# One Softplus activation for the step size of a selective scan, and more outer products on GpSimd

## What is computed

```python
x_dbl = einsum('bsd,ed->bse', u, x_proj_w)           # u: 1024 channels after convolution and silu
dt_r, B, C = split(x_dbl, [64, 80], axis=-1)
dt = softplus(einsum('bsr,dr->bsd', dt_r, dt_proj_w) + dt_proj_b)
A = -exp(A_log)                                       # 1024 x 16
def step(h, inp):                                     # over the tokens
    dt_t, B_t, C_t, u_t = inp
    h = h * exp(dt_t[:, :, None] * A) + (dt_t * u_t)[:, :, None] * B_t[:, None, :]
    y = einsum('bdn,bn->bd', h, C_t)
    return h, y
y = (ys + u * D_param) * silu(z)
x = x + gate * einsum('bse,de->bsd', y, out_proj_w)
```

## Time and profile before

| | |
|---|---|
| median of 3 runs | 2315.27 us |
| lowest and highest run | 2314.59 and 2320.24 us |
| profiled execution: span from first to last instruction | 2313.7 us |
| first layer's units | about 69 to 1815 us of the span |
| TensorE, VectorE, ScalarE, GpSimd busy | 93%, 89%, 69%, 77% |
| granted TensorE clock, mean | 0.96 |

### The profile page before, as it was taken

How to read it: one execution, slowest core, us unless ns; L and a number is a source line. 1 busy time by engine, 2 the same in 40 slices (tenths; PEclk the granted TensorE clock), 3 DMA queues, 4 the chain that set the end, 5 groups by cost and what they waited for, 6 DMA issues and landing times. The chain is left out here.

```text
span 2313.7 us, 30061 instructions
## 1 busy us (share of the span) xinstructions
PE 2147.8 (93%) x9984; PEld 1411.3 (61%) x9984; DVE 2049.7 (89%) x2258; ACT 1607.2 (69%) x3119; POOL 1775.3 (77%) x1048
## 2 busy tenths in 40 slices
PE   9889989988998899899989988998868899999999
PEld 3345555555555555555555555555545599988888
DVE  4899999999999999999999999999999666666666
ACT  3677787887787778777877887787666355566655
POOL 0587899999999999999999999999999422132225
PEclk9889999999999999899999999999978899999999
DMA  6611231151124111421321141114101210112113
GB/s 223 252 39 51 95 134 42 55 175 50 46 52 169 51 55 42 178 91 51 124 99 48 55 178 38 46 54 167 38 22 58 89 35 26 38 57 60 40 55 128
DMA packets 86137, 191.17 MB, mean 83 GB/s; under 512 B 8350, under 2 KB 11678, under 8 KB 85983
## 3 DMA queue, kind: packets, MB, share of 16 engines
q1 hardware_dynamic: 85982, 189.25, 24.7%
HBM read 171.91 MB, written 17.30 MB: 82 GB/s over the span
## 5 line engine op out<-in xcount | busy, mean ns | idle before, releaser
L1460 POOL TENSOR_TENSOR arena<-arena 128x1024 f32<-128x1024 f32 x512 | 1199.9, 2362 | 116.8 <-ACT arena L622 114.7
L1057 DVE TENSOR_TENSOR_SCAN arena<-ps,arena 128x512 f32<-128x512 f32 x1024 | 1240.7, 1258 | 16.5 <-ACT ps L622 13.8
L622 ACT ACTIVATE ps<-arena 128x512 f32<-128x512 f32 x1087 | 717.7, 676 | 276.8 <-DVE arena L1057 190.6
L339 PEld LDWEIGHTS ps<-keep,arena 128*128 128x128 f32 x4096 | 494.8, 147 | 264.0 <-POOL arena L1460 132.7
L339 PE MATMUL ps<-keep,arena 128*128 128x128 f32 x4096 | 551.6, 285 | 94.9 <-POOL arena L1460 89.9
L1042 DVE TENSOR_TENSOR arena<-ps,arena 128x1024 f32<-128x1024 f32 x407 | 491.5, 1208 | 25.2 <-PE ps L339 22.8
L278 PE MATMUL ps<-arena 128*128 128x512 f32 x1024 | 469.1, 604 | 19.3 <-issue 18.6
L278 PEld LDWEIGHTS ps<-arena 128*128 128x128 f32 x1024 | 189.4, 194 | 220.7 <-issue 220.2
L622 ACT ACTIVATE arena<-ps 128x512 f32<-128x512 f32 (+2 forms) x393 | 198.3, 538 | 129.7 <-PE ps L278 63.2
L1427 POOL TENSOR_TENSOR arena<-arena 128x1024 f32<-128x1024 f32 x105 | 247.7, 2359 | 16.6 <-PE ps L339 16.6
L622 ACT ACTIVATE arena<-arena 128x2 f32<-128x2 f32 (+4 forms) x662 | 238.4, 365 | 24.1 <-POOL arena L1404 7.2
(11 more groups left out here) (148 smaller groups left out, 2788.3 us busy)
## 6 DMA issues: line engine op xcount, KB each, us to landing
arena<-scr_bc SPq DMA_DIRECT2D x128, 512.0 KB, 6.9
arena<-in_inT SPq DMA_DIRECT2D x184, 256.0 KB, 2.7
arena<-in_x SPq DMA_DIRECT2D x17, 512.0 KB, 3.6
scr_x<-arena SPq DMA_DIRECT2D x32, 256.0 KB, 2.0
arena_b<-scr_x SPq DMA_DIRECT2D x16, 512.0 KB, 3.7
arena_c<-scr_x SPq DMA_DIRECT2D x32, 256.0 KB, 2.9
out<-arena_c SPq DMA_DIRECT2D x32, 256.0 KB, 2.1
arena<-in_x SPq DMA_DIRECT2D x30, 256.0 KB, 3.5
```

The source lines that it names most:

```text
L339: last = e.matmul(YP[:, 128 * q:128 * q + 128], hb[G % R][:, i, 128 * q:128 * q + 128], ident, start=(g == 0 and i == 0 and q == 0), stop= ...
L622: return e.activation(o_, i_, f, **kw)
L1057: e.tensor_tensor_scan(H, DA[s % 4], H, h0, MUL, ADD).then_inc(v_sc)
L1460: e.tensor_tensor(H, H, Ct[:, GN * g:GN * g + GN, :], MUL).then_inc(g_w)
```

## The change

`softplus` becomes one Softplus activation from PSUM to dt, at step 7 in place of 6, followed by a load of the table set of Exp. Softplus lies in a set of its own, so the build puts a load ahead of it, too. GpSimd's addition goes. dt's readers (`exps`, `du`) and its bank now wait for the one activation (`a_sp`), and the waits that guarded spt move from ScalarE to GpSimd's `du`. The table `pooled` changes. At the start, VectorE's addition of the two parts goes.

```diff
--- before.py
+++ after.py
@@ -146,13 +146,13 @@
...
-        AT = {"dt": 4, "soft": 6, "add": 5, "du": 8, "copy": 12, "yt": 6, "yb": 9, "yf": 13, "proj": (6, 14), "xdbl": (7, 4)}
+        AT = {"dt": 4, "soft": 7, "du": 8, "copy": 12, "yt": 6, "yb": 9, "yf": 13, "proj": (6, 14), "xdbl": (7, 4)}
...
@@ -188,7 +188,7 @@
...
-        pooled = lambda U, g: U > 6 and U != 39 and g in ((1,), (1, 3), (1, 3), (1, 3), (1,), (0, 1, 3), (1, 3), (1, 3))[U % 8]
+        pooled = lambda U, g: U > 6 and U != 39 and g in ((1, 3), (1, 3), (1, 3, 5), (1, 3), (1, 3), (1, 3), (1, 3), (1, 3))[U % 8]
         POOLED = [G for G in range(NU * NG) if pooled(*divmod(G, NG))]
...
@@ -319,7 +319,7 @@
             def dt_mm(U):
                 c, j = divmod(U, 8)
                 e.wait_ge(a_xd, c + 1)
-                P = bank(("dt", U), (a_rl, U) if U else (v_0, 2), 16 * (U - 1) + AT["soft"] + 2 if U else None)
+                P = bank(("dt", U), (a_sp, U + 1), 16 * (U - 1) + AT["soft"] + 2 if U else None)
                 e.matmul(P, wdt[0:65, 128 * j:128 * j + 128], xdbl[c % 2][0:65, :], start=True, stop=True).then_inc(p_dt)
 
             def out_mm(c, n, q, P):
@@ -714,23 +714,12 @@
 
             def softplus(U):
                 e.wait_ge(p_dt, U + 1)
-                if U == 1:
+                if U == 2:
                     e.wait_ge(v_0, 2)
-                elif U:
-                    e.wait_ge(a_du, U - 1)
-                    if ex_no(NG * U):
-                        e.wait_ge(g_ex, ex_no(NG * U))
-                act(spt, BG[bank_of["dt", U]], ACT.Abs).then_inc(a_abs)
-                if U == 2:
-                    e.wait_ge(v_0, 3)
                 elif U > 2:
                     e.wait_ge(g_du, U - 2)
-                if U:
-                    act(dt[U % 2], BG[bank_of["dt", U]], ACT.Relu).then_inc(a_rl)
-                e.wait_ge(a_abs, U + 1)
-                act(spt, spt, ACT.Exp, scale=-1.0).then_inc(a_ex)
-                e.wait_ge(a_ex, U + 1)
-                act(spt, spt, ACT.Ln, bias=1.0).then_inc(a_ln)
+                act(dt[U % 2], BG[bank_of["dt", U]], ACT.Softplus).then_inc(a_sp)
+                e.preload_act_table_set("natural_log_exp_and_others")
 
             def du_copy(U):
@@ -758,7 +747,7 @@
             def exps(s):
                 U, n = divmod(s, 16)
                 if n == 0:
-                    e.wait_ge(*((g_dt, U) if U else (v_0, 2)))
+                    e.wait_ge(a_sp, U + 1)
                 if s >= 4:
                     e.wait_ge(v_sc, s - 3)
                 act(DA[s % 4], dt[U % 2], ACT.Exp, scale=An[:, U % 8, n:n + 1]).then_inc(a_da)
@@ -792,7 +781,7 @@
             x_evac0(7)
             silu_u(0, 6, 7)
             silu_u(0, 7, 8)
-            e.preload_act_table_set("natural_log_exp_and_others")
+            e.preload_act_table_set("softplus")
             proj_evac(0)
             softplus(0)
             e.wait_ge(a_A, 2)
@@ -1034,7 +1023,7 @@
             def expand(G):
                 U, g = divmod(G, NG)
                 if g == 0:
-                    e.wait_ge(*((a_du, U) if U else (v_0, 3)))
+                    e.wait_ge(*((a_du, U) if U else (v_0, 2)))
                 if U % 8 == 0:
                     e.wait_ge(d_B[g], 16 * (U // 8 + 1))
                 if G >= R:
@@ -1104,12 +1093,10 @@
             for i in range(8):
                 taps(i)
 
-            e.wait_ge(a_ln, 1)
-            e.scalar_tensor_tensor(dt[0], BG[bank_of["dt", 0]], 0.0, spt, MAX, ADD).then_inc(v_0)
-            e.wait_ge(v_0, 2)
+            e.wait_ge(a_sp, 1)
             e.wait_ge(a_su, su_of(0))
             e.tensor_tensor(DU, dt[0], u[0][:, 0, :], MUL).then_inc(v_0)
-            e.wait_ge(v_0, 3)
+            e.wait_ge(v_0, 2)
             expand(0)
             scan(0)
             for s in range(NS):
@@ -1408,13 +1395,13 @@
                 e.wait_ge(a_no, 2 * hc)
                 e.tensor_scalar(nmr, sums, -1.0 / 512, None, MUL).then_inc(g_nm)
 
-            def add(U):
-                e.wait_ge(a_ln, U + 1)
-                e.tensor_tensor(dt[U % 2], dt[U % 2], spt, ADD).then_inc(g_dt)
-
             def du(U):
                 c, j = divmod(U, 8)
-                e.wait_ge(g_dt, U)
+                e.wait_ge(a_sp, U + 1)
+                if U > 1:
+                    e.wait_ge(a_du, U - 1)
+                if ex_no(NG * U):
+                    e.wait_ge(g_ex, ex_no(NG * U))
                 e.wait_ge(a_su, su_of(c))
                 e.tensor_tensor(spt, dt[U % 2], u[c % 2][:, j, :], MUL).then_inc(g_du)
@@ -1439,8 +1426,6 @@
                 U, pr = divmod(s, 16)
                 c, j = divmod(U, 8)
                 more = c + 1 < NCH
-                if U + 1 < NU and pr == AT["add"]:
-                    add(U + 1)
                 if U + 1 < NU and pr == AT["du"]:
                     du(U + 1)
                 if s in EXP:
```

More of the change, by code:

```diff
@@ L135, in program @@
             ("ft", "q", "v", "k", "qt", "kt", "kv", "ya", "o"))
-        a_sc, a_A, a_row, a_no, a_xn, a_xh, a_hi, a_e0, a_xq, a_ue, a_du, a_su, a_xd, a_abs, a_ex, a_ln, a_sz, a_da, a_st, a_dg, a_x1, a_sm, a_sq, a_rl = (
-            sem("a_" + n) for n in ("sc", "A", "row", "no", "xn", "xh", "hist", "e0", "xq", "ue", "du", "su", "xd", "abs", "ex", "ln", "sz",
-                                    "da", "st", "dg", "x1", "sm", "sq", "rl"))
+        a_sc, a_A, a_row, a_no, a_xn, a_xh, a_hi, a_e0, a_xq, a_ue, a_du, a_su, a_xd, a_sp, a_sz, a_da, a_st, a_dg, a_x1, a_sm, a_sq = (
+            sem("a_" + n) for n in ("sc", "A", "row", "no", "xn", "xh", "hist", "e0", "xq", "ue", "du", "su", "xd", "sp", "sz",
+                                    "da", "st", "dg", "x1", "sm", "sq"))
         a_wh, a_nx, a_f, a_fh, a_qe, a_qT, a_ek, a_E, a_fc = (sem("a_" + n) for n in ("wh", "nx", "f", "hi", "qe", "qT", "ek", "E", "fc"))
@@ L147, in program @@
                                     "att", "y", "o"))
-        g_c, g_r1, g_r2, g_r3, g_rs, g_nm, g_dt, g_du, g_gw, g_w = (sem("g_" + n) for n in ("c", "r1", "r2", "r3", "rs", "nm", "dt", "du", "gw", "w"))
+        g_c, g_r1, g_r2, g_r3, g_rs, g_nm, g_du, g_gw, g_w = (sem("g_" + n) for n in ("c", "r1", "r2", "r3", "rs", "nm", "du", "gw", "w"))
         g_att, g_m1, g_mask, g_l1, g_l2, g_lrs, g_q, g_xo = (sem("g_" + n) for n in ("att", "m1", "mask", "l1", "l2", "lrs", "q", "xo"))
         after = lambda k, n: ((16 * k[0] + k[1] + n) // 16, (k[1] + n) % 16)
-        AT = {"dt": 4, "soft": 6, "add": 5, "du": 8, "copy": 12, "yt": 6, "yb": 9, "yf": 13, "proj": (6, 14), "xdbl": (7, 4)}
+        AT = {"dt": 4, "soft": 7, "du": 8, "copy": 12, "yt": 6, "yb": 9, "yf": 13, "proj": (6, 14), "xdbl": (7, 4)}
         XMM = {(3, 0): 0, (3, 7): 1, (3, 15): 2, (4, 6): 3, (5, 1): 4, (5, 3): 5, (5, 15): 6, (6, 1): 7}
```

## The result

The changed kernel took 2328.9 us (median of 4 runs, 2323.6 to 2330.5), the kernel before on the same chip 2314.9: a ratio of 1.0054, 95% interval 1.0042 to 1.0066. It is slower by half a per cent, 14 us, where I had forecast no change (2315) and ended my range at 2325. The profiled execution has a span of 2325.8 us, 12.1 above that of before.

A forecast was written before the change was run, and what follows sets the result against it. TensorE was taken to bound the middle of each chunk, VectorE the rest. Span 2313.7 - 8.9 (products) + 4.1 (unit 1) + 5.2 (unit 6) = 2314.1, plus 1.6 as a run: forecast 2315 us, no measurable change, range 2300 to 2325.

The forecast's parts named there:

- Unit 0 is in VectorE's part: seven chunks gain 1.11 each, 7.8 us.: First of a chunk's eight inner-loop turns, where VectorE sets the pace: one product fewer on VectorE gains 7.8 us.
- The cover for GpSimd: Some 9 us between a GpSimd product's turn and its use, so GpSimd falling behind in units 0 and 2 costs nothing.
- Unit 2: Start of TensorE's part of a chunk: the moved product gains nothing in chunks 1 to 6, 1.11 us in chunk 7.
- the 2 us that I gave as a sign: VectorE's wait for TensorE's sums in unit 6 was to grow from 0.95 to about 2 us.
- Unit 4, priced at nothing: One product taken by GpSimd and one given back, so the count stays and no gain or loss was counted.
- Unit 1, 4.1 us: ScalarE's longer step-size block delays an output row and TensorE's z matmul by 0.58 us in seven chunks: 4.1 us lost.
- Unit 6, 5.2 us: Bank planner's changed choice makes the z matmul wait for the convolution's evacuation, 0.87 us in six chunks: 5.2 us lost.
- The block's price: Step size on ScalarE: load, Softplus (0.60 us) and load take 1.1 us more per unit than the four activations' 2.17 us.
- rival C: Each table switch stalls ScalarE for as long again as its load, passed on in units 1, 4 and 6: 2362 us; chance 0.04.
- The sum: Whole kernel: 2313.7 - 8.9 + 4.1 + 5.2 = 2314.1 us of span, 2315.7 us as a run.
- Rival B: Longer wait in unit 1 lowers TensorE's clock; sign: over two z matmuls at 5.37 us; 2324 us, chance 0.16 with unit 6's bound.
- Rival A: VectorE is the limit after all and waits are absorbed: all 15.5 us come through, 2300 us (2304 with half the costs); chance 0.27.

The follow-up runs named there:

- e7: Changed kernel with the dt bank's planned end one step earlier and unit 0's added GpSimd product given back to VectorE: 2320.5 us, ratio 1.0027.
- e8: Changed kernel with the dt bank's planned end one step earlier, a Relu in place of the Softplus and no table loads around it: 2316.1 us, ratio 0.9996.
- e1: Changed kernel with the old table of GpSimd products (105 in place of 119): 2333.5 us, ratio 1.0078.
- e6: Changed kernel with the dt bank's planned end one step earlier and the old table of GpSimd products: 2321.0 us, ratio 1.0027.
- e3: Changed kernel with the dt bank's planned end one step earlier: 2320.4 us, ratio 1.0025.
- e4: Changed kernel with the Softplus at step 6 in place of 7, which also gives back the choice of banks: 2321.1 us, ratio 1.0029.
- e2: Kernel before with the new table of GpSimd products, keeping the old step size of four activations and GpSimd's addition: 2353.8 us, ratio 1.0167.
- e5: Changed kernel with the dt bank's planned end one step earlier and unit 1's output row at step 10 in place of 12: 2305.9 us, ratio 0.9962.
- e9: Kernel before with unit 1's output row on ScalarE at step 10 in place of 12: 2304.3 us, ratio 0.9956.
- e10: Changed kernel with dt bank's planned end one step earlier, output row at step 10, old product table plus three products (units 32, 56, 58): 2306.7 us, ratio 0.9969.
- e11: Kernel before, old step size, with the output row at step 10 and three added GpSimd products (units 32, 56, 58): 2306.9 us, ratio 0.9968.
- e12: Kernel before with unit 1's output row on ScalarE one step later, 13 in place of 12: 2349.5 us, ratio 1.0150.

## Why the prediction was wrong, step by step

- **"Unit 0 is in VectorE's part: seven chunks gain 1.11 each, 7.8 us."** This step failed, and it is the larger part of the miss: the seven units lost 0.7 us, 8.5 of the 11.7 us by which the span missed my sum. The cover for GpSimd was mis-stated: I asked when VectorE uses the product, and not when TensorE needs what is queued behind it. In units 8, 16, 24 and 48 VectorE waited 0.95 to 1.37 us for the sums made late by it. In unit 40 my cover itself was too short, and VectorE waited 3.41 us for the product. Unit 32's 1.12 us came back as a wait in unit 33. By e7 the seven products are worth 0.
- **Unit 2.** Nothing in chunks 1 to 6: right (27.15 and 27.03 us), though the 1.11 us came back as a wait of 0.9 in unit 2 itself and not in unit 6. In unit 46 the wait of 0.95 us stands as before and a new one of 0.83 is added; the two make nearly the 2 us that I gave as a sign, but the second is the bank's and not the product's. Unit 58 gained its 1.13.
- **Unit 4, priced at nothing** since its count stays: lost 0.30 to 0.39 us in each of five chunks and gained 0.37 in unit 36, 1.4 in all. The one taken and the one given back stand at other scans.
- **Unit 1, 4.1 us.** 6.6 measured. What I passed on, 0.58 us of a later row in each of seven chunks, is there: the idle time ahead of the z matmul grew by 0.10 to 0.93 us in each, 4.3 in all. I left out two things. The z matmuls together took 0.9 us more (two of 5.37 us went back to 3.67, and two others rose, to 5.37 and 6.29), and VectorE got new waits for exponentials, 1.95 us in unit 33. By e8, the loads are worth 4.7 us in unit 1.
- **Unit 6, 5.2 us.** Right: the bank, the gap, the wait and the sum (5.6).
- **The block's price.** Right: the load starts at 1347.05, the Softplus at 1348.34 (0.60 us), the second load at 1348.96, the next exponential at 1350.25, 3.20 us in all (3.3 in my sum). The trace has 247 loads, 127 more than before, 1.283 us in the mean. The Trainium skill ("ScalarE: Activation LUTs", What ACT_TABLE_LOAD costs) adds a drain of some 1380 ns to each; this trace shows none, and rival C fell with it.
- **The sum.** With nothing for unit 0, my terms give 2313.7 - 1.1 + 4.1 + 5.2 = 2321.9 us of span, for 2325.8. The rest is mostly unit 1 (2.5) and unit 4 (1.4).
- **Rival B** named a mechanism that is at work in unit 1. By its own sign (more than two slow z matmuls) the changed kernel was not it: it had two in the profiled execution, as before. Other versions were: e1 had seven, e6 and e7 five and six, e3, e4 and e8 three. Which of them turn is not settled by the version alone as far as these traces tell, one execution of each.
- **Rival A** fell: the span grew, so VectorE's 15.8 us all went into waits.

## What to carry to other kernels

Price a moved instruction by the work that is queued behind it on its new engine, and by who waits for that soonest, not only by when its own result is used. Where a planner picks a buffer by a due time, shifting one step of the program can change who waits for whom elsewhere: read the choices again after every shift. And where TensorE stands idle for two microseconds ahead of long matmuls, ask first what sets the length of that gap; here moving one row by two steps gave more than either half of the change could.

## What was not expected of the hardware

- **TensorE's clock after a gap.** In the profiles of before, after, e1, e2, e3, e4, e6, e7 and e8 the z matmul of unit 1 follows 1.6 to 3.7 us without TensorE work. Its first four matmuls took 1.95 us in 31 of 63 cases and 2.80 to 3.75 us in 32. All eleven that followed less than 2.00 us were fast. In units 49 of the changed kernel and of e5, at 1.95 us, the granted clock was 1.00 (the full 2.4 GHz); in unit 33 of the changed kernel it was 0.58 over them, and in unit 57 it was 0.50, the lower level throughout. In e5, e9, e10 and e11 the gap is at most 1.29 us, and all 28 took 1.88 to 1.96 us. In e12 it is 4.8 to 5.0 us, and all seven took 3.46 to 3.75. Between the two, a gap of the same 2.61 us went both ways (1.95 us at a clock of 1.00 and 3.65 us at 0.53, in units 9 and 17 of e6); what decides there stays open.
- **Lateness multiplies.** One step of ScalarE's program is about 1.6 us of scans, yet the row one step later was 3.1 us later, and the seven units 1 of e12 took 34.7 us more, among them 20.2 us more of idle time ahead of the z matmuls and 12.2 us more in these matmuls.
